# First attention written out, with three sequences in flight: scores of one, outputs of its predecessor, projections of its successor

## The chip, the cores and the metric

The kernel runs on one core of one Trainium2 chip. The metric is device microseconds of one execution of the whole program; lower is better. The change touches one stage of seven, the first attention.

## The reference, cut to what matters

x is 8 sequences of 512 rows and 256 columns. The program is a decoder of two layers (attention, cross attention, experts; twice). The stage here is the first attention, with one head whose queries and keys are 64 wide:

```python
def _L0_attn_ref(x, Wq, bq, Wk, bk, Wv, bv):
    Q = jnp.einsum('bsd,de->bse', x, Wq) + bq
    K = jnp.einsum('bsd,de->bse', x, Wk) + bk
    V = jnp.einsum('bsd,de->bse', x, Wv) + bv
    scores = jnp.einsum('bqe,bke->bqk', Q, K)
    attn = jax.nn.softmax(scores, axis=-1)
    attended = jnp.einsum('bqk,bkd->bqd', attn, V)
    return attended + x
...
x = x + _L0_attn_ref(_layernorm(x, axis=-1), L0_attn_Wq, L0_attn_bq, L0_attn_Wk, L0_attn_bk, L0_attn_Wv, L0_attn_bv)
```

## The kernel before, in words

All of x stays in on-chip memory as 32 tiles of 128 rows, 4 to a sequence. `l0_attention` (from L205) is written as one instruction list per engine; each engine works through its list in order, and semaphores carry what is done: `wait_ge(sem, n)` waits for a count, `after` (L24) does so only where the count is above zero. `over_sequences` (L39) writes the body out for sequence 0, loops over 1 to 6, and writes it out again for 7. A body handles sequence b, and begins what sequence b+1 (`nxt`) needs of the layer norm.

The layer norm is the class `Norm`. In `vector_stats` (L91) VectorE takes the statistics of 4 tiles and then does seven small operations; in `gpsimd` (L110) GpSimd takes the power -0.5; in `vector_rows` (L116) VectorE writes the normalised rows `xn`; `tensor` (L128) turns them with 8 transposes on TensorE; in `scalar` (L140) ScalarE copies the turned ones to `xnT`.

TensorE's list for sequence b, in this order:

- query and key (L285): matmuls into one bank of `proj` for each, after all four tiles of the sequence before were added to x (`x_done`). ScalarE takes over the high halves as fp32r (L347, L349), VectorE what is left, the low halves (L376, L379).
- values (L296): into the same two banks of `proj`, the first half after the low half of the query, the second after that of the key. VectorE adds the bias and writes `v1` (L384).
- scores (L307): for each tile t of 128 queries, two matmuls (high and low half of the query) into bank t % 2 of `score`. VectorE takes the negated maximum of each row (L389), and a tile waits for the maximum two tiles back.
- shift row (L313): the four columns of maxima are turned into one row, after all four maxima. ScalarE copies it (L352), VectorE writes its low half (L393).
- transposes of sequence b+1 (L137).
- turned scores (L323 to L325): for each tile of 128 keys, three matmuls (keys by high queries, keys by low queries, ones by shift row). ScalarE takes the exponential into `prob` (L358).
- weighted values (L334): for each tile of queries, products of `prob` with `v1`, whose last column is ones, into bank t % 2 of `proj`. VectorE takes the reciprocal of that column (L396) and adds the product to x (L400).

VectorE's list for b begins with the statistics of b+1; their rows follow the maxima of b. GpSimd adds the normalised rows to x once per sequence (L267), since the attention's residual is its normalised input, and takes the power for b+1 behind it. SyncE loads the weights at the start of the stage and starts one large transfer of zeros for a later stage. `proj`, `score`, `turn` and `shift` fill 7 of the 8 banks of PSUM.

Of the kernel before, what the change touches and what calls it, by code (L numbers as in the profile page):

```python
# [5 lines left out]
ALU = mybir.AluOpType  # L6
ACT = mybir.ActivationFunctionType
# [197 lines left out]
def l0_attention(nc, io, g):  # L205
# [6 lines left out]
    with ExitStack() as ctx:  # L212
# [4 lines left out]
        score = ctx.enter_context(nc.psum_tensor("a0_score", [P, 2, BANK], F32))  # L217
# [5 lines left out]
        qhi, qlo, khl = (sb(n, [P, S], F32R) for n in ("qhi", "qlo", "khl"))  # L223
        v1 = sb("v1", [P, TB, D + 1])
# [33 lines left out]
        def _(pool):  # L258
            pool.memset(v1[:, :, D:D + 1], 1.0).then_inc(ready, 1)
# [3 lines left out]

            def body(b, nxt):

                pool.wait_ge(norm.rows_done, b * TB + TB)
                pool.tensor_tensor(g.x[:, bass.ds(b * TB, TB), :], g.x[:, bass.ds(b * TB, TB), :], norm.xn[:, :, :],  # L267
                                   ALU.add).then_inc(res_done, 1)
                if nxt is not None:
                    norm.gpsimd(nxt)  # L270
            over_sequences(pool, body)

        @block.tensor
        def _(pe):
            pe.wait_ge(loaded, LOADS)
            pe.wait_ge(ready, 3)
            norm.tensor(0)

            def body(b, nxt):

                pe.wait_ge(norm.columns_done, b + 1)
                after(pe, x_done, b * TB)
                for i, w in enumerate((wq2, wk2)):
                    for k in range(KT):
# [4 lines left out]
                for t in range(TB):  # L289
                    if t % 2 == 0:  # L290
                        if t == 0:
                            pe.wait_ge(q_lo, b + 1)
                        else:
                            pe.wait_ge(k_done, b + 1)
                    for k in range(KT):
                        last = pe.matmul(proj[:, t // 2, (t % 2) * D:(t % 2 + 1) * D], norm.xnT[:, k, t * P:(t + 1) * P],  # L296
                                         wv[:, k, :], start=k == 0, stop=k == KT - 1)
                    if t % 2:
                        last.then_inc(v_done, 1)

                for t in range(TB):
                    if t >= 2:
                        pe.wait_ge(max_done, b * TB + t - 1)
                    else:
                        after(pe, exp_done, b * TB + t - 1)
                    for n, q in enumerate((qhi, qlo)):
                        last = pe.matmul(score[:, t % 2, :], q[:, t * P:(t + 1) * P], khl[:, :], start=n == 0, stop=n == 1)  # L307
                    last.then_inc(s_done, 1)

                pe.wait_ge(max_done, b * TB + TB)  # L310
# [4 lines left out]
                if nxt is not None:  # L315
                    norm.tensor(nxt)

                for t in range(TB):
                    if t == 0:
                        pe.wait_ge(shift_lo, b + 1)  # L320
                    if t >= 2:
                        pe.wait_ge(exp_done, b * TB + t - 1)
                    pe.matmul(score[:, t % 2, :], khl[:, t * P:(t + 1) * P], qhi[:, :], start=True, stop=False)  # L323
                    pe.matmul(score[:, t % 2, :], khl[:, t * P:(t + 1) * P], qlo[:, :], start=False, stop=False)
                    pe.matmul(score[:, t % 2, :], ones_r[:, :], shift_hl[:, :], start=False, stop=True).then_inc(st_done, 1)  # L325

                for t in range(TB):
                    if t == 0:
                        pe.wait_ge(v_kept, b * 2 + 2)
                        pe.wait_ge(exp_done, b * TB + TB)  # L330
                    if t >= 2:
# [2150 lines left out]
```

## Time and profile before

| | us |
|---|---|
| three runs | 2740.86, 2730.04, 2725.38 |
| median | 2730.04 |
| the profiled execution | 2746.05 |
| its span, first to last instruction | 2744.1 |
| TensorE busy in the span | 2288.4 (83%) |
| VectorE busy | 1211.4 (44%) |
| ScalarE busy | 671.7 (24%) |
| GpSimd busy | 551.2 (20%) |

The span is one execution as the hardware profiler saw it; 1.95 us of the execution lie outside it. Busy shares are means over stages with different limits, so they say little of one stage. For a stage, the windows view gives each engine's busy time between two moments, with the granted clock of TensorE (1.00 is 2.4 GHz, 0.50 is 1.2 GHz) and the share of the DMA engines. The timeline gives instructions in order of time: start, length, engine, line, what is written from what, how often, and in brackets how long the engine had stood before it and what released it. Matmuls overlap their successors, so the distance between two starts, not the length, tells what one costs.

### The profile page before, as it was taken

How to read it: one execution, taken by the hardware profiler on the slowest of the kernel's cores; microseconds unless marked ns; L12 is line 12 of the kernel's file. 1: busy time of each engine (PE TensorE's matmuls, PEld its weight loads, DVE VectorE, ACT ScalarE, POOL GpSimd, SP SyncE). 2: the span in 40 equal slices, each digit the busy share in tenths (PEclk: the TensorE clock that was granted, in tenths of full speed). 3: DMA queues.
4: the chain of work that ended last, by engine and by line, in shares of the span. 5: the costliest groups of instructions: out<-in, count | busy, mean ns of one | idle time of the engine just before them, and what ended most of it. 6: DMA issues, size and time to landing. Idle time of an engine off the chain costs nothing. (4 is left out here: it accounts for less than half of the span.)

```text
span 2744.1 us, 34995 instructions
## 1 busy us (share of the span) xinstructions
PE 2288.4 (83%) x10514; PEld 1595.4 (58%) x10515; DVE 1211.4 (44%) x3389; ACT 671.7 (24%) x1269; POOL 551.2 (20%) x748
## 2 busy tenths in 40 slices
PE   5887677760599984888888868988899999999998
PEld 3554344460377752555555536776577777777776
DVE  2442777662133335566666534554322222222234
ACT  1211233310011112444444432211122222222211
POOL 1110233217200013333333220011510000000043
PEclk9998899955799995799999989978899999999999
DMA  6000000042122223243333300005410101010033
GB/s 216 0 0 20 0 1 0 0 169 94 66 65 64 63 70 88 61 87 83 83 78 79 63 18 3 5 32 202 146 44 31 34 31 34 31 34 31 27 91 96
DMA packets 122392, 160.36 MB, mean 58 GB/s; under 512 B 21106, under 2 KB 90546, under 8 KB 122034
## 3 DMA queue, kind: packets, MB, share of 16 engines
q1 hardware_dynamic: 110002, 125.53, 16.3%
q0 software_dynamic: 12288, 33.57, 3.9%
q8 instruction: 52, 0.85, 0.1%
q14 instruction: 50, 0.41, 0.1%
HBM read 75.68 MB, written 49.28 MB: 46 GB/s over the span
## 5 line engine op out<-in xcount | busy, mean ns | idle before, releaser
L1437 PE MATMUL e_up_ps<-e_wgu,e_xT 128*128 x1152 | 344.9, 452 | 0.0
L1543 DVE TENSOR_TENSOR e_h<-e_act_g,e_up_ps 128x344 f32<-128x344 f32 x208 | 106.6, 513 | 492.5 <-PE e_ht_ps L1444 407.6
L2027 DVE CUSTOM_DVE_ANT_0 a_s_ps<-a_s_ps,a_causal 128x512 f32<-128x512 f32 (+3 forms) x512 | 241.1, 516 | 111.8 <-PE a_s_ps L1812 110.2
L1437 PEld LDWEIGHTS e_up_ps<-e_wgu,e_xT 128*128 128x128 f32 x1152 | 218.9, 190 | 103.7
L1951 ACT ACTIVATE a_prob<-a_st_ps 128x512 f32<-128x512 f32 (+1 forms) x384 | 197.6, 523 | 286.5 <-PE a_st_ps L1829 282.6
L1470 ACT ACTIVATE e_act_g<-e_up_ps 128x344 f32<-128x344 f32 x208 | 95.2, 458 | 695.5 <-DVE e_h L1543 406.3
L1812 PE MATMUL a_s_ps<-a_ks,a_qs 68*128 68x512 f32 (+3 forms) x512 | 154.5, 368 | 59.5 <-DVE a_most L2027 46.9
L1453 PE MATMUL e_y_ps<-e_wd,e_hT 128*128 x864 | 198.4, 379 | 0.0
L1829 PE MATMUL a_st_ps<-a_qs,a_ks 128*128 128x512 f32 (+3 forms) x512 | 184.7, 411 | 14.0 <-DMA a_qs<-a_m_lo 10.8
L1392 POOL DMA_INDIRECT e_wgu<-slots_y,slot x64 | 60.8, 950 | 661.6 <-DMA slots_y<-e_y 608.6
L1437 PE MATMUL e_up_ps<-e_own_gu,e_xT 128*128 128x344 f32 x512 | 164.3, 477 | 19.3 <-DVE e_xT L1483 13.8
L1718 POOL TENSOR_SCALAR_AFFINE_SELECT a_prob<-a_prob 128x256 f32<-128x256 f32 x256 | 101.9, 422 | 353.0 <-ACT a_prob L1951 350.5
L1453 PEld LDWEIGHTS e_y_ps<-e_wd,e_hT 128*128 128x128 f32 x864 | 158.5, 190 | 18.6
L1829 PEld LDWEIGHTS a_st_ps<-a_qs,a_ks 128*128 128x128 f32 x512 | 94.8, 200 | 103.4 <-ACT a_prob L1951 42.8
L1812 PEld LDWEIGHTS a_s_ps<-a_ks,a_qs 68*128 68x128 f32 x512 | 98.5, 204 | 94.2 <-DVE a_most L2027 71.0
L1437 PEld LDWEIGHTS e_up_ps<-e_own_gu,e_xT 128*128 128x128 f32 x512 | 102.0, 201 | 72.9 <-DVE e_xT L1483 15.5
L1139 PE MATMUL e_h_ps<-e_w,e_xT 128*128 x288 | 137.1, 599 | 2.9 <-DVE e_xT L1173 2.9
L1154 PE MATMUL e_y_ps<-e_w,e_hT 128*128 x576 | 136.1, 379 | 0.0
L1165 ACT ACTIVATE e_hT<-e_ht_ps 128x512 f32<-128x512 f32 x72 | 43.0, 597 | 367.9 <-PE e_ht_ps L1145 367.9
L1122 PE MATMUL e_xt_ps<-ident,e_xin 128*128 128x128 f32 x144 | 27.8, 275 | 103.8 <-DMA e_xin<-slots_x 103.8
L1154 PEld LDWEIGHTS e_y_ps<-e_w,e_hT 128*128 128x128 f32 x576 | 103.9, 190 | 11.2
L1841 PE MATMUL a_o_ps<-a_prob,a_v 128*32 128x512 f32 (+3 forms) x1024 | 100.6, 469 | 1.4 <-POOL a_prob L1718 1.4
(384 smaller groups left out, 3762.4 us busy)
## 6 DMA issues: line engine op xcount, KB each, us to landing
e_xin<-slots_x SPq DMA_DIRECT2D x144, 128.0 KB, 2.0
slots_y<-e_y SPq DMA_DIRECT2D x144, 128.0 KB, 1.7
slots_x<-zero_row SPq DMA_DIRECT2D x1, 9216.0 KB, 27.2
e_w<-in_L_ffn_w SPq DMA_DIRECT2D x16, 512.0 KB, 9.8
a_qs<-a_hi SPq DMA_DIRECT2D x32, 256.0 KB, 4.9
a_ks<-a_hi SPq DMA_DIRECT2D x32, 256.0 KB, 5.1
a_qs<-a_lo SPq DMA_DIRECT2D x32, 256.0 KB, 6.1
a_ks<-a_lo SPq DMA_DIRECT2D x32, 256.0 KB, 7.1
```

What stands on the lines that cost most here:

```text
L1139: last = pe.matmul(h_ps[:, j, :], xT[:, j, k * P:(k + 1) * P], w1[:, e, k, :], start=k == 0, stop=k == KT - 1)
L1154: last = pe.matmul(y_ps[:, j, 0:D], hT[:, j, c * P:(c + 1) * P], w2[:, e, c, :], start=c == 0, stop=c == C - 1)
L1437: last = pe.matmul(up_ps[:, 2 * half_ + u_, 0:H], xT[:, j, k * P:(k + 1) * P], up[:, k, u_, half_ * H:(half_ + 1) * H], start=k == 0, stop ...
L1453: last = pe.matmul(y_ps[:, 0:D], hT[:, j, c * P:(c + 1) * P], down[:, c, :], start=c == 0, stop=c == C - 1)
L1470: act.activation(act_g[:, :], up_ps[:, 2 * half_, 0:H], ACT.Silu).then_inc(gated, 1)
L1543: dve.tensor_tensor(h[:, half_ * H:(half_ + 1) * H], act_g[:, :], up_ps[:, 2 * half_ + 1, 0:H], ALU.mult).then_inc(h_kept, 1)
L1718: below = lambda two: pool.affine_select(out=two, in_=two, compare_op=ALU.is_ge, fill=0.0, base=0, pattern=[[0, 2], [1, P]], channel_multi ...
L1812: last = pe.matmul(s_ps[:, u % 2, off:off + (t + 1) * P], qs[0:ROW_M, head, t * P:(t + 1) * P], ks[0:ROW_M, head, 0:(t + 1) * P], start=Tr ...
L1829: last = pe.matmul(st_ps[:, u % 2, off:off + S - t * P], ks[:, head, t * P:(t + 1) * P], qs[:, head, t * P:], start=True, stop=True)
L1841: last = pe.matmul(o_ps[r:r + 2 * HD, t * P:], v[:, t, gr * GH + h, :], prob[:, gr % 2, h, K_AT[t]:K_AT[t] + S - t * P], start=t == 0, sto ...
L1951: act.activation(prob[:, gr % 2, u // 3, (u % 3) * BANK:(u % 3) * BANK + cols], st_ps[:, u % 2, 0:cols], ACT.Exp).then_inc(exp_done, 1)
L2027: last = dve.tensor_tensor_reduce(s_ps[:, u % 2, off:off + cols], s_ps[:, u % 2, off:off + cols], causal[:, S - cols:], 1.0, -3.0e38, ALU. ...
```

## The change

Instead of one body per sequence with a loop, every engine's list is written out in Python for all sequences, as `for b in range(B + 1)`. In round b the scores and the shift row are those of sequence b, the weighted values and the additions to x those of b-1, and query, key and values those of b+1; VectorE also takes the statistics and the rows of b+2. TensorE's list in a middle round is: scores 0 and 1 of b; transposes of b+1; weighted 0 of b-1; score 2; weighted 1; score 3; weighted 2 and 3; shift row of b; query and key of b+1; turned scores 0 and 1; first half of the values of b+1; turned score 2; second half; turned score 3. Query, key and values get a second buffer (`b % 2`), and `score` a third bank, so that all 8 banks are in use.

The core of the diff (removed lines are those of the functions printed above):

```diff
-        score = ctx.enter_context(nc.psum_tensor("a0_score", [P, 2, BANK], F32))
+        score = ctx.enter_context(nc.psum_tensor("a0_score", [P, 3, BANK], F32))
...
-        qhi, qlo, khl = (sb(n, [P, S], F32R) for n in ("qhi", "qlo", "khl"))
-        v1 = sb("v1", [P, TB, D + 1])
+        qhi, qlo, khl = (sb(n, [P, 2, S], F32R) for n in ("qhi", "qlo", "khl"))
+        v1 = sb("v1", [P, 2, TB, D + 1])
...
+            def query_and_key(b):
                 pe.wait_ge(norm.columns_done, b + 1)
                 for i, w in enumerate((wq2, wk2)):
+                    after(pe, x_done, (b - 2) * TB + TB - 1 + i)
...
+            def scores(b, t):
+                pe.wait_ge(q_lo, b + 1)
+                pe.wait_ge(k_done, b + 1)
+                if t < 3:
+                    after(pe, exp_done, (b - 1) * TB + t + 2)
+                else:
+                    pe.wait_ge(max_done, b * TB + t - 2)
+                for n, q in enumerate((qhi, qlo)):
+                    last = pe.matmul(score[:, (8 * b + t) % 3, :], q[:, b % 2, t * P:(t + 1) * P], khl[:, b % 2, :], start=n == 0, stop=n == 1)
+                last.then_inc(s_done, 1)
+
...
+            def turned_scores(b, t):
+                pe.wait_ge(shift_lo, b + 1)
+                if t == 3:
+                    pe.wait_ge(exp_done, b * TB + 1)
+                u, keys = (8 * b + 4 + t) % 3, khl[:, b % 2, t * P:(t + 1) * P]
+                pe.matmul(score[:, u, :], keys, qhi[:, b % 2, :], start=True, stop=False)
+                pe.matmul(score[:, u, :], keys, qlo[:, b % 2, :], start=False, stop=False)
+                pe.matmul(score[:, u, :], ones_r[:, :], shift_hl[:, :], start=False, stop=True).then_inc(st_done, 1)
+
+            def weighted(b, t):
+                pe.wait_ge(v_kept, b * 2 + 2)
+                pe.wait_ge(exp_done, b * TB + TB)
+                if t < 2:
+                    after(pe, v_kept, (b + 1) * 2 + t + 1 if b + 1 < B else 0)
+                else:
+                    pe.wait_ge(x_done, b * TB + t - 1)
+                for j in range(TB):
+                    last = pe.matmul(proj[:, t % 2, 0:D + 1], prob[:, j, t * P:(t + 1) * P], v1[:, b % 2, j, :],
+                                     start=j == 0, stop=j == TB - 1)
+                last.then_inc(o_done, 1)
+
+            norm.tensor(0)
+            query_and_key(0)
+            for i in range(2):
+                value(0, i)
+            for b in range(B + 1):
+                if b < B:
+                    scores(b, 0)
+                    scores(b, 1)
+                if b + 1 < B:
+                    norm.tensor(b + 1)
                 for t in range(TB):
+                    if b > 0:
+                        weighted(b - 1, t)
+                    if b < B and t < 2:
+                        scores(b, t + 2)
+                if b < B:
+                    shift_row(b)
+                    if b + 1 < B:
+                        query_and_key(b + 1)
+                    for t in range(TB):
+                        turned_scores(b, t)
+                        if b + 1 < B and t in (1, 2):
+                            value(b + 1, t - 1)
...
+            query_and_key(0)
+            for b in range(B):
+                if b + 1 < B:
+                    norm.scalar(b + 1, free=[(v_done, b * 2 + 2)])
                 act.wait_ge(shift_done, b + 1)
                 after(act, st_done, b * TB)
                 act.activation(shift_hl[0:1, :], shift[0:1, :], ACT.Copy).then_inc(shift_hi, 1)
+                if b + 1 < B:
+                    query_and_key(b + 1)
                 for t in range(TB):
                     act.wait_ge(st_done, b * TB + t + 1)
                     after(act, o_done, b * TB)
+                    act.activation(prob[:, t, :], score[:, (8 * b + 4 + t) % 3, :], ACT.Exp).then_inc(exp_done, 1)
...
+            query_and_key(0)
+            dve.wait_ge(g.x_rest, 16)
+            norm.vector_stats(1)
+            for i in range(2):
+                value(0, i)
+            norm.vector_rows(1, free=[(res_done, 1)])
+            for b in range(B + 1):
+                if b < B:
+                    maximum(b, 0)
+                    maximum(b, 1)
                 for t in range(TB):
+                    if b > 0:
+                        add_to_x(b - 1, t)
+                    if b < B and t < 2:
+                        maximum(b, t + 2)
+                if b < B:
+                    dve.wait_ge(shift_hi, b + 1)
+                    dve.tensor_tensor(shift_hl[32:33, :], shift[0:1, :], shift_hl[0:1, :].bitcast(F32), ALU.subtract).then_inc(shift_lo, 1)
+                if b + 1 < B:
+                    query_and_key(b + 1)
+                    if b + 2 < B:
+                        norm.vector_stats(b + 2)
+                    for i in range(2):
+                        value(b + 1, i)
+                    if b + 2 < B:
+                        norm.vector_rows(b + 2, free=[(res_done, b + 2)])
```

On GpSimd, `norm.gpsimd(1)` now stands before the loop and `norm.gpsimd(b + 2)` behind the residual addition of b.

## Rows read from the trace of the kernel before

**Rows 1.** Windows, one sequence each: start:end, length, busy per engine, clock, DMA share, GB/s

```profile
87.73:114.39 26.66, 23.35 (x93) 15.09 (x93) 12.22 (x33) 5.38 (x8) 3.39 (x2) 1.00 0.00 0
141.04:169.34 28.30, 25.00 (x92) 16.29 (x93) 12.16 (x33) 5.38 (x8) 3.38 (x2) 0.94 0.00 0
222.73:253.35 30.62, 26.50 (x84) 16.70 (x84) 8.66 (x17) 4.35 (x7) 0.00 (x0) 0.83 0.00 1
```

**Rows 2.** Timeline of TensorE, one middle sequence: start us, us, what, [idle before]

```profile
87.73 1.98 PE L285 MATMUL a_proj<-a_xnT,a_wq 128*128 128x512 f32 x4 [0.89 <-DVE x_rows L400]
...
91.47 3.72 PE L296 MATMUL a_proj<-a_wv,a_xnT 128*128 128x256 f32 x16
94.84 0.58 PE L307 MATMUL a_score<-a_khl,a_qhi 128*128 128x512 f32 x1
95.25 0.39 PE L307 MATMUL a_score<-a_khl,a_qlo 128*128 128x512 f32 x1
95.48 0.39 PE L307 MATMUL a_score<-a_khl,a_qhi 128*128 128x512 f32 x1
...
98.68 1.03 PE L313 MATMUL a_shift<-ident,a_negmax 128*1 128x128 f32 x8 [0.78 <-DVE a_negmax L389]
99.65 1.09 PE L137 MATMUL a_turn<-ident,a_xn 128*128 128x128 f32 x8
101.11 0.50 PE L323 MATMUL a_score<-a_qhi,a_khl 128*128 128x512 f32 x1 [0.37 <-DVE a_shift_hl L393]
...
102.20 0.50 PE L323 MATMUL a_score<-a_qhi,a_khl 128*128 128x512 f32 x1
...
106.30 7.20 PE L334 MATMUL a_proj<-a_v,a_prob 128*128 128x257 f32 x32 [0.78 <-ACT a_prob L358]
```

**Rows 3.** Timeline of the other engines beside rows 2

```profile
87.67 1.41 DVE L94 BATCH_NORM_STATS2 a_stats<-x_rows 128x6 f32 x4
...
89.84 0.69 ACT L347 ACTIVATE a_qhi<-a_proj,a_bq 128x512 fp32r<-128x512 f32 x1 [10.33 <-PE a_proj L285]
...
90.20 1.02 POOL L114 TENSOR_TENSOR a_rstd<-a_var_eps,minus_half 128x4 f32<-128x4 f32 x1 [14.38 <-DVE a_var_eps L108]
...
90.66 0.75 DVE L376 SCALAR_TENSOR_TENSOR a_qlo<-a_proj,a_bq,a_qhi 128x512 fp32r<-128x512 f32 x1 [0.63 <-ACT a_qhi L347]
...
95.22 0.69 DVE L384 TENSOR_TENSOR a_v<-a_proj,a_bv 128x512 f32<-128x512 f32 x1 [1.03 <-PE a_proj L296]
...
97.34 1.29 DVE L389 TENSOR_REDUCE a_negmax<-a_score 128x1 f32<-128x512 f32 x2 [0.23 <-PE a_score L307]
...
98.55 1.37 DVE L125 TENSOR_SCALAR a_xn<-x_rows,a_mean,a_rstd 128x256 f32 x4
...
100.11 2.37 POOL L267 TENSOR_TENSOR x_rows<-x_rows,a_xn 128x1024 f32 x1 [8.89 <-DVE a_xn L125]
...
105.56 0.60 ACT L358 ACTIVATE a_prob<-a_score 128x512 f32<-128x512 f32 x1 [0.49 <-PE a_score L325]
...
108.64 0.48 DVE L400 SCALAR_TENSOR_TENSOR x_rows<-a_proj,a_rinv,x_rows 128x256 f32 x1 [0.16 <-DVE a_rinv L396]
...
110.38 0.48 DVE L400 SCALAR_TENSOR_TENSOR x_rows<-a_proj,a_rinv,x_rows 128x256 f32 x1 [0.16 <-DVE a_rinv L396]
```

**Rows 4.** Timeline, first sequence of the stage

```profile
38.87 0.76 DVE L379 SCALAR_TENSOR_TENSOR a_khl<-a_proj,a_bk,a_khl 64x512 fp32r<-64x512 f32 x1 [1.35 <-ACT a_khl L349]
...
41.33 0.58 PE L307 MATMUL a_score<-a_khl,a_qhi 128*128 128x512 f32 x1
...
45.17 1.03 PE L313 MATMUL a_shift<-ident,a_negmax 128*1 128x128 f32 x8 [0.78 <-DVE a_negmax L389]
...
47.60 0.50 PE L323 MATMUL a_score<-a_qhi,a_khl 128*128 128x512 f32 x1 [0.36 <-DVE a_shift_hl L393]
```

**Rows 5.** Timeline, end of the last sequence of the stage

```profile
242.66 9.96 PE L334 MATMUL a_proj<-a_v,a_prob 128*128 128x257 f32 x32 [0.78 <-ACT a_prob L358]
...
252.87 0.48 DVE L400 SCALAR_TENSOR_TENSOR x_rows<-a_proj,a_rinv,x_rows 128x256 f32<-128x256 f32 x1
```

More of the change, by code:

```diff
@@ L287, in body, with value, shift_row @@
                     last.then_inc(qk_done, 1)
[L289 to L294, printed above, removed]
+            def value(b, i):
+                pe.wait_ge((q_lo, k_done)[i], b + 1)
+                for t in (2 * i, 2 * i + 1):
                     for k in range(KT):
-                        last = pe.matmul(proj[:, t // 2, (t % 2) * D:(t % 2 + 1) * D], norm.xnT[:, k, t * P:(t + 1) * P],
+                        last = pe.matmul(proj[:, i, (t % 2) * D:(t % 2 + 1) * D], norm.xnT[:, k, t * P:(t + 1) * P],
                                          wv[:, k, :], start=k == 0, stop=k == KT - 1)
[L298 to L308, printed above, removed]
+                last.then_inc(v_done, 1)
+            def scores(b, t):
[8 more added lines that the diff above has]
+                last.then_inc(s_done, 1)
+            def shift_row(b):
                 pe.wait_ge(max_done, b * TB + TB)
@@ L327, in body @@
[L327 to L331, printed above, removed]
-                        pe.wait_ge(x_done, b * TB + t - 1)
-                    for j in range(TB):
-                        last = pe.matmul(proj[:, t % 2, 0:D + 1], prob[:, j, t * P:(t + 1) * P], v1[:, j, :],
-                                         start=j == 0, stop=j == TB - 1)
-                    last.then_inc(o_done, 1)
@@ L366, in _, with query_and_key @@
             dve.wait_ge(loaded, LOADS)
[L368 to L372 removed]
+            def query_and_key(b):
                 dve.wait_ge(q_hi, b + 1)
[L375 to L376 removed]
+                after(dve, st_done, (b - 1) * TB)
+                dve.scalar_tensor_tensor(out=qlo[:, b % 2, :], in0=proj[:, 0, :], scalar=bq2[:, 0:1], in1=qhi[:, b % 2, :].bitcast(F32),
@@ L386, in body @@
-                for t in range(TB):
-                    dve.wait_ge(s_done, b * TB + t + 1)
-                    after(dve, shift_done, b)
-                    dve.tensor_reduce(negmax[:, t:t + 1], score[:, t % 2, :], AX.X, ALU.max, negate=True).then_inc(max_done, 1)
-                if nxt is not None:
-                    norm.vector_rows(nxt, free=[(res_done, b + 1)])
-                dve.wait_ge(shift_hi, b + 1)
-                dve.tensor_tensor(shift_hl[32:33, :], shift[0:1, :], shift_hl[0:1, :].bitcast(F32), ALU.subtract).then_inc(shift_lo, 1)
@@ L402, in _, with value @@
-            over_sequences(dve, body)
+                dve.scalar_tensor_tensor(out=khl[H:P, b % 2, :], in0=proj[H:P, 1, :], scalar=bk2[H:P, 0:1],
+                                         in1=khl[H:P, b % 2, :].bitcast(F32), op0=ALU.add, op1=ALU.subtract).then_inc(k_done, 1)
+            def value(b, i):
+                dve.wait_ge(v_done, b * 2 + i + 1)
+                after(dve, o_done, (b - 1) * TB)
+                dve.tensor_tensor(v1[:, b % 2, 2 * i:2 * i + 2, 0:D], proj[:, i, :].rearrange("p (t d) -> p t d", t=2),
+                                  bv[:, :].unsqueeze(1).broadcast_to([P, 2, D]), ALU.add).then_inc(v_kept, 1)
@@ new lines, in maximum, with add_to_x @@
+            def maximum(b, t):
+                dve.wait_ge(s_done, b * TB + t + 1)
+                after(dve, shift_done, b)
+                dve.tensor_reduce(negmax[:, t:t + 1], score[:, (8 * b + t) % 3, :], AX.X, ALU.max, negate=True).then_inc(max_done, 1)
+            def add_to_x(b, t):
+                dve.wait_ge(o_done, b * TB + t + 1)
+                dve.reciprocal(rinv[:, t:t + 1], proj[:, t % 2, D:D + 1]).then_inc(rinv_done, 1)
+                dve.wait_ge(rinv_done, b * TB + t + 1)
+                dve.wait_ge(res_done, b + 1)
+                xt = g.x[:, b * TB + t, :]
+                dve.scalar_tensor_tensor(out=xt, in0=proj[:, t % 2, 0:D], scalar=rinv[:, t:t + 1], in1=xt,
+                                         op0=ALU.mult, op1=ALU.add).then_inc(x_done, 1)
```

63 lines of the change are left out of this document (12 added, 51 removed).

## The prediction

> **What bounds the kernel now.** I read first the busy time of each engine by stretches, cut at the first projection matmul of each sequence. A middle sequence of the stage takes 26.66 us, and in it TensorE is busy for 23.35, VectorE for 12.22, ScalarE for 5.38 and GpSimd for 3.39 [rows 1]. So no engine but TensorE comes near the length of the block, and the DMA share is zero: loads play no part. Then I read TensorE in order of time through one such block [rows 2] and the other three beside it [rows 3]. The reader is to see that TensorE does seven pieces one after another, and that after most of them it stands while one short chain of another engine ends: a maximum, the shift, the last exponential, the last addition to x. Prices of the pieces, start to start: query and key 3.74 (87.73 to 91.47, with a short wait in it); values 3.37 (to 94.84); scores: the first of the eight matmuls took 0.41, the following ones 0.23 each (95.25 to 95.48), so 0.41 + 7 x 0.23 = 2.0; shift row 0.97 (98.68 to 99.65); transposes 1.0 (1.09 with the drain of the last); turned scores 4 x 1.09 = 4.36 (101.11 to 102.20 is one); weighted values 4 x 1.74 = 6.96 (the additions to x follow each other by 110.38 - 108.64) [rows 2, 3]. The sum is 22.4 us. The other 4.2 us of the block are waits. That is what the change can win in each block, and everything below asks how much of it.
>
> **Part by part.**
>
> *Order on TensorE.* Work per sequence is the same: no matmul is added or dropped. I lay the pieces of a middle block at the prices above, zero being the first score. Two scores end at 1.0, transposes 2.0, weighted(b-1,0) 3.75, score 4.4, weighted 6.15, score 6.8, weighted 8.55 and 10.3, shift row 11.3, query and key of b+1 15.0, two turned scores 17.2, value half 18.9, turned 20.0, value half 21.7, turned 22.8. Now each wait is held against this. An addition ends 0.75 after its weighted tile (reciprocal, then 0.48 for the addition): 4.5, 6.9, 9.3, 11.05. Weighted tiles 2 and 3 need the first two (6.8, 8.55: met), query needs the third (11.3: met), key the fourth (13.1: met). A maximum takes 0.65 (half of 1.29): the last one ends at 7.55, the shift row asks for it at 10.3. The chain from the start of the shift row to the first turned score took 2.43 [rows 2], so it ends at 12.7, asked for at 15.0. High half of the query 0.69, low half 0.75: ready at 14.8, asked for by the values at 17.2; of the key at 16.6, asked for at 20.0. Statistics of b+2 then run from 16.6; from their start to the end of GpSimd's power are 3.55 (87.67 to 90.20, and 1.02), so at 20.2 [rows 3]. Value halves are taken over in 0.69 each, the second by 22.55; the rows of b+2 (1.37) follow until 24.0. **The one tight place** is there: the transposes of b+2 start in the next block at 1.0, which is 24.0 on this clock, and follow tile by tile. The last exponential (0.60) ends 0.75 after the last turned score, and the first weighted tile asks for it 2 us later. The third score bank takes away the wait of a score for the maximum two tiles back, and of the next block's scores for the last exponentials.
>
> *Doubled buffers* for queries, keys and values cost no instruction; they let the writes of b+1 go ahead while b is read. I price them at nothing.
>
> *GpSimd and SyncE.* The residual addition (2.37) still follows the normalised rows, now beside the maxima of the next block rather than the shift; x is wanted with it at 3.9, and it ends by 1.0 + 0.2 + 2.4 = 3.6 after the rows of the block before, and belongs to a later sequence anyway. No DMA is moved; SyncE's list is untouched.
>
> *Switches.* TensorE now changes between plain f32 and fp32r groups ten times per sequence (before: four, three of them behind a wait). The only switch without a wait in front is values to scores: 0.41 against 0.23, or 0.18 more [rows 2]. My sum holds one; nine more cost between nothing and 1.6 us. The turned scores are priced with their slow entries in, and the weight loads of a group may run ahead, so I take a third, 0.6. **Period 23.0**, with 22.4 and 24.0 as its ends.
>
> *Written out.* Six bodies leave the loop. The first sequence is straight code before too: from first score to first turned score it took 47.60 - 41.33 = 6.27, the looped one 101.11 - 94.84 = 6.27 [rows 2, 4]. So straight code costs nothing that shows. The Trainium skill, "Runtime: NRT & Kernel Launch", section "Instruction fetch mechanics", says that straight code is fetched ahead in blocks, mostly hidden, and that a taken branch to a place outside what is held stalls; by it the written-out stage would lose nothing, and the equal 6.27 agree as far as they go.
>
> *The start gets worse.* The statistics of sequence 1 now stand behind the key's low half, which ends at 39.63 [rows 4], where before they stood ahead of the query's low half. Statistics end at 42.0, the two value takeovers at 43.4, the rows at 44.8, transposes 45.1; the maxima stand behind the rows and end at 47.4, the shift row starts at 47.55 (before 45.17, the same piece), query and key of 1 end at 52.25, turned scores and values 7.75 later, with switches at 60.3.
>
> *Sum.* 60.3, then six blocks of 23.0 = 198.3. The eighth has no successor: scores, weighted tiles of 6 and switches 9.4, shift chain 2.43 uncovered, turned scores 4.36: 214.5. Its outputs: wait 0.78, matmuls 7.20, tail 0.9: **223.4**. Before, the last addition ended at 252.87 + 0.48 = 253.35 [rows 5]. Gain 30 us.
>
> *Clock.* Some of that 30 was a fallen clock before. One middle block took 28.30 at a granted clock of 0.94, the last block has 0.83 [rows 1]; its weighted matmuls took 9.96 instead of 7.20 [rows 2, 5], which is what a stretch at 1.2 instead of 2.4 GHz does. That is 1.64 + 2.76 = 4.4 us at least. Both falls come in blocks with 0.78 and more of standing still before the last group. In the new order such gaps are left in the first and the last block only. I count no fall in the new kernel; if the same price stays, 4.4 are lost again. The Trainium skill, "TensorE: Matmul & The Clock Gate", section "HAM oscillation — how this bites in real kernels", says that idle gaps which come back in every round of a loop make the clock fall again in every round; by that rule every block before would be paid at the lower level, and closing the gaps would win that too. The granted clock of 1.00 in the first block of rows 1, which has all its gaps, speaks against it, so I count nothing for the clock in the other blocks.
>
> *Against which time.* The profiled execution took 2746.05 us (span 2744.1), so it would come to 2716. It lies 16 above the median of 2730.04. The falls may be missing in the median run, which takes up to 4.4 off the gain; I take 28: **2702**.
>
> **Rivals.**
>
> *The tight place does not hold* (chance 0.15). If the rows of b+2 come 1.5 to 2 us later than laid out, because VectorE has a longer list than I gave it, transposes, the copy of them and the maxima all move, and the block gets 25 us. For it: one engine in order now carries two sequences, and 1.0 against 1.0 is no slack. Against it: 12.2 busy of 23, and the four adjoining places have 2 us of slack each. Gain 30 - 7 x 2 = 16: 2714.
>
> *It changes nothing that can be measured* (0.07). The stage still runs one sequence at a time, since some handover that I took as early is late, such as the first score waiting for an exponential of the block before, and the waits have only changed places; or the written-out code stalls where the loop didn't. Then the 4.2 us stay in each block, and the worse start of 2.4 is added: 2728 to 2732. Against it: every wait above has a time.
>
> *Slower* (0.03). TensorE pays more for each change of kind than the one bare row shows. 63 more changes stand against 34 us (30 and the 4 counted for them): it decides from 0.54 us each. If each cost what TensorE stood before the shift row, 0.78 [rows 2], that is 49 us and a loss of 15: 2745. Against it: 0.18 where it can be seen.
>
> *Denser than laid out* (0.15). Weight loads run ahead over the switches, the period is 22.4 and the clock holds: gain 34: 2695.
>
> **How the numbers follow.** The forecast as laid out has 0.60. Under 0.5% (13.7 us) a measurement of this kernel can't tell from no change: its three runs span 15 us. Faster by more than that is below 2716.4: forecast and denser case whole (0.75), and two thirds to three quarters of the first rival (0.11): 0.86. The same: the rest of the first rival and the second, 0.11. Slower: 0.03. The range: low end from a gain of 34 and the runs' own scatter of some 8: 2688. High end from a period of 24.0 (7 less), the clock falling as before (4.4 less), so a gain near 18 and the scatter: 2720.
>
> **What would show it.** In the changed profile, the blocks between first scores should be 22.4 to 24 us apart; TensorE's idle time before the weighted values, the shift row, and query and key should be gone in blocks 1 to 6, with about 1.4 us of shift chain left in the last. The transposes may show a wait for the rows of at most 0.3. The first block should show a wait of about 1.5 for the rows and another of 1 for the maxima. VectorE's share of a block goes from 46% to 53%. The stage should end near 223. I am wrong if blocks take over 25 us, if the next stage starts later than 235, or if the gaps before f32 groups behind fp32r ones exceed 0.4.

## The result and the profile after

| | before | after |
|---|---|---|
| median of four runs each | 2730.87 us | 2705.81 us |
| lowest to highest | 2725.38 to 2740.86 | 2702.93 to 2708.66 |
| profiled execution: span | 2744.1 | 2706.9 |
| stage of the change, end of the last addition to x | 253.35 | 221.29 |

The ratio is 0.990, with a 95% interval of 0.9864 to 0.9937: 25 us faster by the medians, 27 by the ratio, 17 to 37 by the interval. The forecast was 2702 us with a range of 2688 to 2720. Two further measurements of the same kernel on other chips gave 0.9901 (0.9866 to 0.9936) and 0.9873 (0.9839 to 0.9908); these are 27 and 35 us by the ratio, 28 and 32 by the medians.

First the windows of the changed kernel: two middle blocks from first score to first score, the first block, and the end of the stage (columns as in [rows 1]).

```profile
64.29:86.36 22.07, 22.07 (x93) 15.40 (x92) 12.21 (x33) 5.37 (x8) 3.35 (x2) 1.00 0.00 0
86.36:108.44 22.08, 22.08 (x93) 15.39 (x92) 12.20 (x33) 5.37 (x8) 3.36 (x2) 1.00 0.00 1
41.50:64.29 22.79, 18.52 (x63) 10.37 (x61) 11.73 (x33) 4.78 (x7) 6.68 (x4) 0.85 0.53 187
196.00:221.29 25.29, 22.40 (x95) 16.18 (x93) 9.04 (x22) 3.57 (x6) 0.00 (x0) 1.00 0.00 1
```

A middle block takes 22.08 us instead of 26.66, and TensorE is busy in all of it. VectorE, ScalarE and GpSimd are busy for as long as before [rows 1]. The first block has a granted clock of 0.85 and TensorE idle for over 4 us.

The timeline of TensorE through one middle block of the changed kernel answers to [rows 2]:

```profile
86.36 0.50 PE L301 MATMUL a_score<-a_khl,a_qhi 128*128 128x512 f32 x1
...
87.40 1.04 PE L137 MATMUL a_turn<-ident,a_xn 128*128 128x128 f32 x8
88.27 1.91 PE L328 MATMUL a_proj<-a_v,a_prob 128*128 128x257 f32 x8
89.83 0.58 PE L301 MATMUL a_score<-a_khl,a_qhi 128*128 128x512 f32 x1
90.24 0.39 PE L301 MATMUL a_score<-a_khl,a_qlo 128*128 128x512 f32 x1
90.47 1.90 PE L328 MATMUL a_proj<-a_v,a_prob 128*128 128x257 f32 x8
...
96.26 1.03 PE L308 MATMUL a_shift<-ident,a_negmax 128*1 128x128 f32 x8
97.22 1.98 PE L281 MATMUL a_proj<-a_xnT,a_wq 128*128 128x512 f32 x4
...
100.36 0.80 PE L316 MATMUL a_score<-a_qhi,a_khl 128*128 128x512 f32 x1
...
102.82 1.99 PE L289 MATMUL a_proj<-a_wv,a_xnT 128*128 128x256 f32 x8
104.47 0.58 PE L316 MATMUL a_score<-a_qhi,a_khl 128*128 128x512 f32 x1
...
108.44 0.50 PE L301 MATMUL a_score<-a_khl,a_qhi 128*128 128x512 f32 x1
```

No row has a bracket, so there is no wait left. The reader should compare starts. From one weighted tile to the next with a score between them (88.27 to 90.47) there are 2.20 us, and that is 1.74 for the tile and 0.46 for a score's two matmuls, no more. The other engines beside it answer to [rows 3]:

```profile
86.31 1.38 DVE L125 TENSOR_SCALAR a_xn<-x_rows,a_mean,a_rstd 128x256 f32<-128x256 f32 x4
...
87.61 1.28 DVE L407 TENSOR_REDUCE a_negmax<-a_score 128x1 f32<-128x512 f32 x2
...
105.90 2.37 POOL L266 TENSOR_TENSOR x_rows<-x_rows,a_xn 128x1024 f32<-128x1024 f32 x1
...
107.66 0.69 DVE L401 TENSOR_TENSOR a_v<-a_proj,a_bv 128x512 f32<-128x512 f32 x1 [2.11 <-PE a_proj L289]
...
108.40 0.73 DVE L125 TENSOR_SCALAR a_xn<-x_rows,a_mean,a_rstd 128x256 f32<-128x256 f32 x2
```

The tight place of the prediction is in the last rows: the rows of b+2 begin at 108.40, 0.04 before the next block, and the transposes at 109.48 don't wait for them. GpSimd's residual addition, over at 108.27, is wanted by these rows too (`res_done`) and comes 0.13 before them. The prediction did not have this second tight edge. It had the addition end 3.6 us into a block; here it starts 19.5 us in (105.90 less 86.36), behind the power for b+2.

The first block and the end, beside [rows 4] and [rows 5]:

```profile
39.05 0.76 DVE L395 SCALAR_TENSOR_TENSOR a_khl<-a_proj,a_bk,a_khl 64x512 fp32r<-64x512 f32 x1 [1.69 <-ACT a_khl L365]
...
42.27 1.01 POOL L114 TENSOR_TENSOR a_rstd<-a_var_eps,minus_half 128x4 f32<-128x4 f32 x1 [18.18 <-DVE a_var_eps L108]
...
43.25 2.33 POOL L266 TENSOR_TENSOR x_rows<-x_rows,a_xn 128x1024 f32<-128x1024 f32 x1
45.72 1.38 DVE L125 TENSOR_SCALAR a_xn<-x_rows,a_mean,a_rstd 128x256 f32<-128x256 f32 x4 [2.21 <-POOL x_rows L266]
46.28 1.32 PE L137 MATMUL a_turn<-ident,a_xn 128*128 128x128 f32 x8 [3.49 <-DVE a_xn L125]
...
50.06 1.86 PE L308 MATMUL a_shift<-ident,a_negmax 128*1 128x128 f32 x8 [0.78 <-DVE a_negmax L407]
```

```profile
213.37 7.20 PE L328 MATMUL a_proj<-a_v,a_prob 128*128 128x257 f32 x32 [0.78 <-ACT a_prob L380]
...
220.81 0.48 DVE L415 SCALAR_TENSOR_TENSOR x_rows<-a_proj,a_rinv,x_rows 128x256 f32<-128x256 f32 x1
```

### The profile page after: what moved, and what is told of

Same layout as the page of the kernel before. It is cut to its first block and busy times, and to the rows that moved or that the text cites. A ratio compares the mean times of both kernels' runs of the same rounds, so it can differ in the third digit from the quotient of the medians.

```text
span 2706.9 us, 34780 instructions
## 1 busy us (share of the span) xinstructions
PE 2289.5 (85%) x10514; PEld 1602.9 (59%) x10515; DVE 1212.1 (45%) x3389; ACT 671.5 (25%) x1269; POOL 549.7 (20%) x748
## 5 line engine op out<-in xcount | busy, mean ns | idle before, releaser
L1163 PE MATMUL e_xt_ps<-ident,e_xin 128*128 128x128 f32 x144 | 28.1, 277 | 102.1 <-DMA e_xin<-slots_x 102.1
L1882 PE MATMUL a_o_ps<-a_prob,a_v 128*32 128x512 f32 (+3 forms) x1024 | 107.6, 498 | 1.4 <-POOL a_prob L1759 1.4
```

The source lines that it names most:

```text
L1882: last = pe.matmul(o_ps[r:r + 2 * HD, t * P:], v[:, t, gr * GH + h, :], prob[:, gr % 2, h, K_AT[t]:K_AT[t] + S - t * P], start=t == 0, sto ...
```

## The experiments

**The kernel before, again.**

> The kernel before, once more, for a second trace. If the falls of TensorE's clock in the stage belong to the order of its work, they come back: a last block of about 30.6 us and a stage that ends near 253. If they are a matter of the moment, the stage ends at 247 to 249 (253.35 less the 4.4 to 5.9 us that the falls cost), middle blocks stay at 26.66 us, and 4 to 6 us of the 32 by which the two profiled executions differ in this stage are not the change's.

Middle blocks were 26.65 all through, so the fall of the clock in one of them was of the moment. In the last block it fell once more:

```profile
242.28 10.01 PE L334 MATMUL a_proj<-a_v,a_prob 128*128 128x257 f32 x32 [0.78 <-ACT a_prob L358]
```

From the last shift row to the last addition, the last block took 19.88 us in the first profiled execution (233.47 to 253.35) and 21.32 in this one, where the changed kernel at full clock takes 15.53 for the same work (205.76 to 221.29), and so does the old order written out, below. So the falls in the first execution cost 4.35 and 1.64, 6.0 us in all, and the stage's gain of 32 is made of these 6 and of 26 us from the new order.

The stage ended at 253.01. Behind it, this execution was 20.6 us shorter than the first: from the first statistics of the last stage to the end of the span are 2723.2 - 1808.59 = 914.6 us, where the first profiled execution had 2744.1 - 1808.83 = 935.3. So the two spans of the result can't simply be subtracted: of their 37.2 us, 32.2 lie in this stage and 20.6 in the last one, which the change doesn't touch (the changed kernel has 914.7 there, like this execution); second attention and second cross attention give back 18.1 (768.5 to 786.6), the rest is 2.6.

**Written out, in the old order.**

```diff
-            over_sequences(pe, body)
+            for b in range(B):
+                body(b, b + 1 if b + 1 < B else None)
```

and the same on the other three engines.

> The kernel before with its four loops of this stage written out, the order of all work unchanged. My theory: the gain comes from the order alone, so the blocks stay at 26.6 us and the time at that of the kernel before, within 2 us; VectorE's addition after a reciprocal starts 0.1 us earlier, at most 0.1 us per block on the path. Rival: writing out gives part of the gain by itself; then blocks under 26 us and a time 5 us or more below.

The ratio was 1.0006 (0.9982 to 1.0031), the median 2732.5. Undisturbed blocks took 26.42 instead of 26.66: a quarter of a microsecond per block, more than the 0.1 expected, and 1.4 us in all, against 4.58 us per block for the whole change. So the shorter block comes from the order. The falls of the clock took other places: every second block, four in all, took about 28.1 us at a granted clock of 0.94, the last block kept the full clock, and the stage ended at 251.90.

**GpSimd in the old order.**

```diff
             norm.gpsimd(0)
-            norm.gpsimd(1)
             for b in range(B):
...
-                if b + 2 < B:
-                    norm.gpsimd(b + 2)
+                if b + 1 < B:
+                    norm.gpsimd(b + 1)
```

> The changed kernel, with GpSimd's power for the next sequence behind the residual addition of its own, as before the change, instead of two sequences ahead. Theory: in the first block the rows of sequence 1 waited for the residual addition, which stood behind a power that had to wait for late statistics; with the order turned, the rows start at 43.5 instead of 45.7, TensorE's wait before the transposes falls from 3.49 to about 1.3 us, and the stage ends 2 us sooner at the least; if the clock no longer falls at 46, up to 6 us sooner (about 215 to 219). Middle blocks stay at 22.1. Rival: VectorE's own list (two value takeovers ahead of the rows) sets the moment; then the rows still start at 45 or later and nothing is won.

The cause was right. The timeline of this kernel:

```profile
42.33 1.02 POOL L114 TENSOR_TENSOR a_rstd<-a_var_eps,minus_half 128x4 f32<-128x4 f32 x1 [14.46 <-DVE a_var_eps L108]
43.49 1.37 DVE L125 TENSOR_SCALAR a_xn<-x_rows,a_mean,a_rstd 128x256 f32<-128x256 f32 x4
44.04 1.32 PE L137 MATMUL a_turn<-ident,a_xn 128*128 128x128 f32 x8 [1.19 <-DVE a_xn L125]
...
47.31 0.93 PE L307 MATMUL a_shift<-ident,a_negmax 128*1 128x128 f32 x7 [1.00 <-DVE a_negmax L406]
```

The rows begin at 43.49 instead of 45.72, TensorE waits 1.19 instead of 3.49 before the transposes, and the shift row comes 2.75 us earlier. The last shift row of the stage came 4.81 us earlier (200.95 for 205.76). But nearly nothing of it arrived at the end of the stage, 220.74 against 221.29, and the expected 215 to 219 were missed:

```profile
210.73 9.29 PE L327 MATMUL a_proj<-a_v,a_prob 128*128 128x257 f32 x32 [0.78 <-ACT a_prob L379]
```

The clock did not fall in the first block any more; it fell in the last, where the weighted values took 9.29 instead of 7.20, and all from the last shift row on 19.79 instead of 15.53. The ratio was 0.9895 (0.986 to 0.9929), not to be told from the changed kernel's.

**Statistics of sequence 1 early as well.**

```diff
-            query_and_key(0)
             dve.wait_ge(g.x_rest, 16)
             norm.vector_stats(1)
+            query_and_key(0)
```

> As the GpSimd order above, and VectorE takes the statistics of sequence 1 ahead of the query's low half, as before the change. Theory: the rows then wait only for the value takeovers, start near 43.2, and together with the early power the first block loses little against the old one; TensorE's wait before the transposes about 1 us, stage end 0.3 to 1 us before the run above. Rival: early statistics push the low halves of the first query back by 2.3 us and give it back there; then no gain or a loss of up to 1 us beside the run above.

The transposes waited 0.28, the shift row came at 46.75, another 0.56 sooner, and the low halves of the first query were not late. The clock fell in the last block again:

```profile
209.46 10.16 PE L327 MATMUL a_proj<-a_v,a_prob 128*128 128x257 f32 x32 [0.78 <-ACT a_prob L379]
```

The stage ended at 220.34, the ratio was 0.9891 (0.9858 to 0.9925). A shift row that came 3.3 us earlier in the first block (46.75 for 50.06) left 1 us at the end of the stage.

**The changed kernel, again.**

> The changed kernel once more, for a second trace and a narrower ratio. Stage of the change: ends near 222, middle blocks 22.08. The traces so far put 32 us of gain into this stage, and the runs show 25 to 28 of the whole program. Theory: the rest is given back in the stages behind, whose granted clock falls at other places (second attention and second cross attention together 787 us against 768 and 771). If that belongs to the change, this trace has 778 to 790 there again; if it is chance, 768 to 772 come as often.

Blocks took 22.08, the stage ended at 219.21, and the ratio was 0.9901. Second attention and second cross attention together took 790.2 us in this trace, at the upper edge of the 778 to 790 expected if the time belongs to the change, and far from the 768 to 772 of chance; in the third trace of the changed kernel, further below, they took 786.7. But chance is not excluded by that: the variants in this document, whose code in these stages is the same, took 773.9 to 793.7, the old order written out 781.1, and the kernel before has only two traces, with 768.5 and 770.8. Whether the time belongs to where the stages begin is asked by the padded kernel below.

**Projections alone.** TensorE's list for b becomes: four scores, transposes, shift row, query and key of b+1, turned scores with the value halves between them, then the weighted values of b itself; VectorE's in the same way.

```diff
+            for b in range(B):
+                for t in range(TB):
+                    scores(b, t)
+                if b + 1 < B:
+                    norm.tensor(b + 1)
+                shift_row(b)
...
+                for t in range(TB):
+                    weighted(b, t)
```

> Half of the change: query, key and values of the successor stand between the shift row and the turned scores, as in the changed kernel, but the weighted values of a sequence follow its own turned scores, as before. By my rows the waits for the query's low half (0.2), before the turned scores (0.4) and before query and key (0.9 to 1.1) go, those in the scores and before the shift row (1.6) and before the weighted values (0.8) stay: blocks of 24.4 to 25.0 us, stage end near 240, time 10 to 17 us under the kernel before. Rival: the waits only move and a block keeps 26 us or more; then the two halves of the change work only together.

This came out better than expected: blocks of 23.39, a stage end of 234.78, a ratio of 0.9924 (0.9898 to 0.995), which is 21 us. The timeline of TensorE:

```profile
143.68 1.04 PE L137 MATMUL a_turn<-ident,a_xn 128*128 128x128 f32 x8
144.83 1.03 PE L308 MATMUL a_shift<-ident,a_negmax 128*1 128x128 f32 x8
...
157.86 7.20 PE L328 MATMUL a_proj<-a_v,a_prob 128*128 128x257 f32 x32 [0.73 <-issue]
164.71 0.58 PE L301 MATMUL a_score<-a_khl,a_qhi 128*128 128x512 f32 x1
...
168.23 1.03 PE L308 MATMUL a_shift<-ident,a_negmax 128*1 128x128 f32 x8
```

The transposes now stand between the scores and the shift row and cover the last maxima: 1.15 us from their start to the shift row, of which 0.3 at most is a wait (87.40 to 88.27 is 0.87 without one). The third score bank takes the wait between the second and third score. I had left both with the other half of the change. What is left is the wait of 0.73 before the weighted values, these 0.3, and a fourth score that starts 0.24 late. So the projections with these two make 3.27 of the 4.58 us, and the overlap with the predecessor's outputs 1.31.

**Two score banks.**

```diff
-        score = ctx.enter_context(nc.psum_tensor("a0_score", [P, 3, BANK], F32))
+        score = ctx.enter_context(nc.psum_tensor("a0_score", [P, 2, BANK], F32))
```

with the waits for `exp_done` and `max_done` one tile closer.

> The changed kernel with two score banks instead of three. The first score of a block must wait for the exponential two tiles back and the second for the last one, which ends 0.7 us after its matmuls. Theory: TensorE stands 0.3 to 0.6 us in each block, blocks 22.4 to 22.7, 2 to 4 us over the changed kernel. Rival: the third bank is what makes the order work, and a score waits for the maximum that stands behind additions to x in VectorE's list; then blocks of 23.5 us or more.

Blocks took 22.43, 0.35 more, as expected; the ratio was 0.9894 (0.9856 to 0.9932). In this order the third bank is worth 2.5 us of the stage, which the program's time doesn't show.

**Late rows.**

```diff
                     if b + 2 < B:
+                        for n in range(2):
+                            dve.tensor_reduce(spare[:, 2 * b + n:2 * b + n + 1], wv[:, :, :].rearrange("p k e -> p (k e)"), AX.X, ALU.max)
                         norm.vector_rows(b + 2, free=[(res_done, b + 2)])
```

> The changed kernel with two reductions over 512 columns (about 1.3 us of VectorE, their results unused) ahead of the rows of b+2, the place that I called tight. In the trace the rows begin 0.05 us before the next block and the transposes 1.04 after it, tile by tile. Theory: there is 0.4 to 0.8 us of slack, so a block grows by 0.5 to 0.9 us, once, to 22.6 to 23.0: stage end 3 to 6 us later. Rival one: VectorE still has room (12 of 22 us) and nothing moves. Rival two: the lateness runs on through maxima and additions and each block grows by the whole 1.3 us.

Blocks took 22.89, 0.81 more, in the expected band; the ratio was 0.9921 (0.9899 to 0.9944). The stage ended at 228.00, 6.7 us later instead of 3 to 6; the clock fell in its last block too, which took 19.92 us from the shift row on instead of 15.53. The timeline of one block:

```profile
130.22 1.27 DVE L445 TENSOR_REDUCE a_spare<-a_wv 128x1 f32<-128x512 f32 x2
...
131.40 1.38 DVE L125 TENSOR_SCALAR a_xn<-x_rows,a_mean,a_rstd 128x256 f32<-128x256 f32 x4
...
131.96 1.32 PE L137 MATMUL a_turn<-ident,a_xn 128*128 128x128 f32 x8 [0.37 <-DVE a_xn L125]
```

The two reductions push the rows back by 1.2 us, the transposes wait 0.37 and run at the pace of the rows. So 0.4 us was the slack at the place that the prediction called tight. No other place was delayed for comparison.

**Full rows.** The run with early statistics, with

```diff
-        shift_hl = sb("shift_hl", [H, S], F32R)
-        ones_r = sb("ones_r", [H, P], F32R)
+        shift_hl = sb("shift_hl", [P, S], F32R)
+        ones_r = sb("ones_r", [P, P], F32R)
```

> The run with early statistics, and the shift row and the ones that multiply it stand in 128 partitions instead of 64; the 64 more are zeros, so the product is the same. In every trace a turned score's three matmuls start 0.34, 0.32 and 0.42 us apart, where three scores of the same width start 0.23 apart. Theory: the load of 64 rows of weights between loads of 128 rows isn't run ahead, and costs 0.1 us before and behind; with 128 rows throughout the three take 0.7 instead of 1.09, a block 22.08 - 4 x 0.3 to 0.39 = 20.5 to 20.9, the stage ends 9 to 12 us sooner. Rival: the spacing comes from accumulating three products in one bank or from the kind of operands, not from the number of rows; then nothing changes.

Blocks took 20.53 us, 1.55 less, and the stage ended at 202.71. That is 17.6 us sooner than with early statistics, and outside the expected 9 to 12: 10.8 of it lie between first and last shift row, 1.1 in an earlier start, and 5.7 behind the last shift row, of which 1.5 are the last four turned scores and the rest mostly the fallen clock that the run with early statistics had there. One thing in the expectation is not so: the 64 added rows of the shift row hold zeros, but those of the ones that multiply it hold ones. The product is the same. Before, the three matmuls of a turned score started 0.34, 0.32 and 0.42 apart in the middle blocks ([rows 2] has two starts of a whole group, 1.09 apart). Now, in the second execution of this kernel:

```profile
92.01 0.40 PE L316 MATMUL a_score<-a_qlo,a_khl 128*128 128x512 f32 x1
92.25 0.39 PE L317 MATMUL a_score<-a_shift_hl,a_ones_r 128*128 128x512 f32 x1
92.48 0.40 PE L315 MATMUL a_score<-a_qhi,a_khl 128*128 128x512 f32 x1
92.72 0.39 PE L316 MATMUL a_score<-a_qlo,a_khl 128*128 128x512 f32 x1
```

They are 0.24, 0.23 and 0.24 apart. The weight loads (PEld) show the difference. First three of the changed kernel, then one of the second execution with full rows:

```profile
101.32 0.18 PEld L318 LDWEIGHTS a_score<-a_shift_hl,a_ones_r 64*128 64x128 f32 x1 [0.37 <-issue]
101.74 0.19 PEld L316 LDWEIGHTS a_score<-a_qhi,a_khl 128*128 128x128 f32 x1 [0.24 <-issue]
101.85 0.19 PEld L317 LDWEIGHTS a_score<-a_qlo,a_khl 128*128 128x128 f32 x1
```

```profile
92.02 0.19 PEld L317 LDWEIGHTS a_score<-a_shift_hl,a_ones_r 128*128 128x128 f32 x1
```

The load of 128 rows behind 128 rows starts 0.22 us ahead of its matmul (101.85 for 102.07), while the matmul before it runs. The load of 64 rows starts with its matmul (101.32), and so does the load of 128 rows behind it (101.74). With full rows this load too runs ahead (92.02 for 92.25). The Trainium skill, "TensorE: Matmul & The Clock Gate", section "Part 3: Packing small matmuls — row/col tiling", says in its list of what overlaps that a weight load overlaps a running matmul only where the row groups differ; by that alone none of these loads would be hidden, since all use the lower rows. The traces disagree: 128 rows behind 128 rows keep a distance of 0.23 although each load takes 0.19. The same section also lets a load be pulled ahead when it goes to the background weight buffer, and that fits these loads. That the change between 64 and 128 rows stops this is what the loads above show. It costs 0.38 us per group of three: 1.09 less the 0.71 of now. The ratio was 0.9796 (0.9754 to 0.9839) on a chip on which the kernel before took 2758.66, so it was measured once more beside the changed kernel.

> The changed kernel beside the run with full rows on one chip, so that the two can be compared with each other. Ratio to the kernel before 0.988 to 0.991, as in the two measurements so far, on whatever chip.

> The run with full rows once more. Its stage is 12 us shorter than that of the run with early statistics by 7 blocks of 1.55, and 1 to 5 more against the changed kernel; the one measurement had 20 us and more on top of that against the kernel before. Theory: what the stage's trace shows is what the program gains, 13 to 17 us under the changed kernel, ratio to before about 0.984 to 0.986, and the rest was that chip's scatter. Rival: 128 rows keep TensorE's clock up further on, and 25 us stand again.

On one chip the changed kernel took 2700.04, ratio 0.9873 (0.9839 to 0.9908), and full rows 2689.97, ratio 0.9839 (0.9805 to 0.9872). The stages ended at 218.80 and 203.30, so there are 15.5 us in the stage and 10 in the medians. Both expectations were missed narrowly: the first ratio by 0.0007, and of the 13 to 17 us of the second only 10 came. The rival's 25 us did not come again. In the stage full rows are 15.5 us better than the changed kernel; for the program the two intervals overlap, so its gain over the changed kernel is not shown there.

**Padded.** The changed kernel, and behind VectorE's last addition in the stage

```diff
+            for n in range(48):
+                dve.tensor_reduce(spare[:, n:n + 1], wv[:, :, :].rearrange("p k e -> p (k e)"), AX.X, ALU.max)
```

> The changed kernel, with 48 reductions of VectorE (their results unused) behind its last addition to x in the stage: about 31 us in which nothing else runs, so that all later stages begin where they began before the change, and take 31 us longer in all if they are indifferent to when they begin. Theory one: the falls of the clock behind the stage are chance; the time is 2705 to 2708 and 31 = 2736 to 2739, level with the kernel before. Theory two: the later stages do better at their old place, which is why the runs show 27 us where the stage's traces show 32 to 34; then 2729 to 2733, and second attention and second cross attention together take 768 to 772 us again.

The next stage began at 251.08, 3 us before its old place. The ratio was 0.9995 (0.9964 to 1.0027), 2759.44 beside 2758.66 of the kernel before on the same chip. That is level, as theory one has it, but the interval is 9 us to either side and holds theory two's time as well. The trace decides more: second attention and second cross attention took 785.7 us, as in the three traces of the changed kernel without padding (786.6, 790.2, 786.7), and not 768 to 772. So putting these stages back to their old place does not bring their old time back, and theory two fails. What makes them longer than in the two traces of the kernel before stays open.

## Why the prediction was right, and where it was off

*The bound.* This was right. TensorE is busy for 22.08 of 22.08 us, and with all its waits gone the block has become the sum of its pieces.

*The period.* The forecast was 23.0 with ends at 22.4 and 24.0; measured were 22.08, below the low end. Two terms were mis-sized. The switches were priced at 0.6 us, from the one start of 0.41 behind values; they cost nothing. The weighted tile that a score follows takes 1.56 instead of 1.74 (88.27 to 89.83), and the score's first start is longer by the same 0.18: a change of kind shifts 0.18 us from one group's row to the next. Reading the one side alone made a cost of it. And query and key were priced at 3.74 with a wait in it; without, 97.22 to 100.36, they take 3.14 and the first turned score 0.3 more.

*The overlap.* On TensorE, VectorE and ScalarE it was right step by step. With the first score at zero, the prediction had the shift row at 10.3 and query and key at 11.3; they started at 9.90 and 10.86. No addition, maximum or low half was late. The run with late rows shows 0.4 us to spare at the one place named as tight.

*GpSimd.* This is the step that failed. The prediction named only what GpSimd's residual addition runs beside, not what it stands behind. GpSimd works in order; `norm.gpsimd(1)` came to stand ahead of the addition of sequence 0, and with it the addition waited for statistics that VectorE had moved back. The addition ran at 43.25 instead of 25.7, and the rows of sequence 1 waited for it until 45.72 (forecast 43.4). The shift row came at 50.06, forecast 47.55; the run with GpSimd in the old order gave 47.31. The middle blocks have the same displacement: the forecast end of the addition, 3.6 us into a block, is what the run with the old order has (104.92 + 2.35, less a first score at 103.65), and the changed kernel starts it at 19.5. There it cost nothing, because the rows of b+2 came 0.13 us later still.

*The clock.* "I count no fall in the new kernel" was wrong in each of its three traces: the clock fell in the first block, behind the wait of 3.4 to 3.5 us before the transposes. The first blocks took 22.79, 21.06 and 21.13 us against 17.92 in the run with GpSimd's old order; 2.2 to 2.3 of that is the longer wait, so the fall cost 0.9 to 2.6 us. The last block kept the full clock in all three. With GpSimd's old order, and with early statistics too, the first block kept it and the last one did not; with late rows and with the projections alone both fell, with full rows neither, in two executions; in the old order written out it was every second block. What decides between these isn't shown. The fall in the last block before was also dearer than its 2.76: 4.35 us, as the prediction's "at least" allows. The Trainium skill's section that the prediction sets against its count ("TensorE: Matmul & The Clock Gate", "HAM oscillation — how this bites in real kernels") is about idle gaps several times as long as the 0.4 to 1.1 us that recur in a block before, so it does not carry over to those blocks, and a granted clock of 1.00 in nearly all of them is no evidence against it.

*The sum.* The forecast for the end of the stage was 223.4, measured were 221.29 (219.21 and 218.80 in the other two): the six blocks were priced 6 x 0.92 = 5.5 us too dear, the last 0.6, and the first score of block 1 came 4.0 us later than laid out (64.29 for 60.3). That these errors cancel to 2.1 us is luck. The gain of the stage was 32 to 34.5 us instead of 30. For the program I took 28, for the falls that a median run may lack; 27, 27 and 35 were measured by the ratio. The three intervals all hold 32 (ratio 0.9883), so the times show no loss behind the stage. The traces do: second attention and second cross attention, which the prediction counted at nothing, took 15 to 22 us more in all four traces with the changed stage (the padded one included) than in the two of the kernel before. If that is typical of the kernel before, about half of the stage's gain is given back there; the times of the program speak against it, two traces do not decide it, and the cause stays open.

*The rivals.* The tight place held. "Nothing that can be measured" is excluded by the blocks of 22.08 us, and its straight-code branch by the old order written out. "Slower" needed a price for each change of kind, and the ten changes together cost nothing that shows. "Denser than laid out" came true for the period alone: the clock did not hold in the first block, and the program took 2705.81, not 2695. Its reason isn't shown either: at the change of kind at 104.47 the weight load starts 0.03 us ahead of its matmul, inside a group of 128 rows 0.22.

## What to carry to other kernels

Where one engine does nearly all the work of a stage in several dependent pieces, lay its pieces of two or three neighbours between one another, price them start to start, and hold every other engine's chain against that list, the queue of each engine included: what is put ahead of an instruction on an idle engine is as much a delay as on a busy one. Before taking a price for a change of kind from one row, look whether the neighbouring row is shorter by the same amount. When TensorE is full, look at matmuls of unlike heights between its weight loads.

## What the runs showed of the hardware that was not expected

- An fp32r matmul over 64 rows between ones over 128 rows cost 1.09 - 0.71 = 0.38 us for each group of three, because its load and the one behind it did not start ahead; filling the operands to 128 rows (zeros in one, ones in the other) took it away, 1.55 us of a 22.08 us block.
- Changing between plain f32 and fp32r ten times per block costs nothing that shows.
- Taking out a wait does not by itself win back a fallen clock: with the first block's wait gone, the last block's weighted values took 9.29 and 10.16 us instead of 7.20 in two executions. In the two with full rows they took 7.20.
- The same instructions in the untouched last stage took 914.6 to 914.9 us in eleven of the fourteen traces and 935.3, 936.7 and 939.1 in three. Two of these three are the traces from the chip on which the kernel before had its highest median, 2759 us against 2731 to 2736 on the others. In the second tenth of the stage the granted clock was 0.91 or 0.89 in those three, and 0.96 in the two shorter ones that were compared. A difference between two profiled spans says little of a change in one stage; the stage's own rows do.
